# Moving the copy of the finished attention chunk out of PSUM from VectorE to ScalarE, in a fused attention and feed-forward kernel

## What is computed

```python
q = rope((x @ Wq + bq).reshape(B, T, 16, 64))
k, v = split(((x @ Wdown + bdown) @ Wup + bup).reshape(B, T, 16, 128))
att = softmax(einsum('bthd,btgd->bthg', q, rope(k)) / 8)      # heads h against heads g
out = einsum('bthg,btgd->bthd', att, v).reshape(B, T, 1024)
x = layernorm(x + out @ Wout + bout)
h = silu(x @ wg.T) * (x @ wu.T)                               # hidden size 3072, int weights / 127
x = layernorm(x + h @ wd.T)
```

## Time and profile before

| | us |
|---|---|
| time, median of 2 runs | 3666.14 (3661.13 to 3671.15) |
| the profiled execution: its time | 3658.49 |
| its span (core 7, the slowest) | 3656.6 |
| spans of the 8 cores | 3622.4 to 3656.6 |
| mean granted TensorE clock of the cores | 0.904 to 0.915 |

### The profile page before, as it was taken

The page is one execution under the profiler, slowest core; times in us unless marked ns, Lnnn a source line. Parts: engine busy times, 40 slices in busy tenths (PEclk is TensorE's granted clock), DMA queues, the critical chain, the costliest instruction groups (busy, mean ns, idle before and its releaser), DMA issues.

```text
span 3656.6 us, 41977 instructions; the slowest of 8 cores (3622.4 to 3656.6 us)
## 1 busy us (share of the span) xinstructions
PE 2749.2 (75%) x12672; PEld 1091.5 (30%) x12672; DVE 1726.1 (47%) x2582; ACT 768.6 (21%) x1349; POOL 292.1 (8%) x540
## 2 busy tenths in 40 slices
PE   0000686779887989698978997898879897989576
PEld 0000222233333333333333333333333333333222
DVE  1221446465546545654546364645565446545312
ACT  0000310133123220413040403231233113220101
POOL 0111000001000110011001100010001100110010
PEclk9999756699998999899999999899999998999778
DMA  6887100202232223222231224122322322222222
GB/s 186 241 240 198 34 1 24 58 29 64 87 78 67 67 93 76 72 59 87 71 91 50 78 74 111 35 62 92 81 67 64 93 61 70 67 87 69 87 72 84
DMA packets 108705, 303.97 MB, mean 83 GB/s; under 512 B 16192, under 2 KB 24768, under 8 KB 108496
## 3 DMA queue, kind: packets, MB, share of 16 engines
q1 hardware_dynamic: 61520, 169.14, 16.3%
q0 software_dynamic: 46976, 132.15, 12.3%
HBM read 269.77 MB, written 39.85 MB: 85 GB/s over the span
## 4 chain that ended last, share of the span: by engine, by line
PE 61%; DMA 9%; DVE 9%; issue 6%; ACT 4%; DVEq 0%; ACTq 0%; POOLq 0%; POOL 0%; SPq 0%
PE P L448 10%; PE P L395 9%; PE P L405 9%; PE P L731 9%; PE P L747 8%; PE P L644 7%; PE P L585 3%; DMA wgb<-wg_s 3%; DVE p_sb L696 3%; DMA wub<-wu_s 3%; PE P L344 2%; DMA wqb<-wq_s 2%; PE P L785 2%; DVE esum L670 2%; DVE hadb L619 1%
## 5 line engine op out<-in xcount | busy, mean ns | idle before, releaser
L696 DVE TENSOR_TENSOR p_sb<-P,vdup 128x512 bf16<-128x512 f32 x1024 | 698.4, 690 | 366.7 <-PE P L747 328.3
L395 PE MATMUL P<-x_bf,wgb 128*128 128x512 bf16 x1536 | 521.7, 409 | 106.7 <-DMA wub<-wu_s 85.9
L405 PE MATMUL P<-x_bf,wub 128*128 128x512 bf16 x1536 | 517.7, 406 | 18.3 <-DVE h_sb L421 18.2
L731 PE MATMUL P<-e_sb,selz_sb 16*128 16x512 bf16 x1024 | 427.2, 425 | 130.0 <-DVE e_sb L680 68.8
L448 PE MATMUL P<-h_sb,wdb 128*128 128x512 bf16 x1536 | 501.2, 391 | 19.6 <-DVE r_bf L457 19.0
L747 PE MATMUL P<-p_sb,id_sb 128*128 128x256 bf16 x2048 | 494.2, 299 | 24.1 <-DVE p_sb L696 17.9
L619 DVE TENSOR_TENSOR hadb<-q_sb,krep 128x2048 bf16<-128x2048 bf16 x256 | 310.0, 1224 | 373.2 <-PE P L644 284.8
L644 PE MATMUL P<-hadb,selred_sb 128*16 128x256 bf16 x2048 | 321.8, 276 | 42.4 <-DVE hadb L619 19.3
L311 PE MATMUL P<-x_bf,wd_sb 128*128 128x512 bf16 x128 | 38.9, 459 | 358.8 <-DMA x_bf<-xt 358.6
L414 ACT ACTIVATE s_sil<-P 128x512 bf16<-128x512 f32 x192 | 114.4, 596 | 921.9 <-PE P L395 921.3
L421 DVE TENSOR_TENSOR h_sb<-s_sil,P 128x512 bf16<-128x512 bf16 x192 | 130.5, 680 | 320.7 <-PE P L405 274.8
(11 more groups left out here) (69 smaller groups left out, 1936.0 us busy)
## 6 DMA issues: line engine op xcount, KB each, us to landing
wdb<-wdn_s SPq DMA_DIRECT2D x64, 768.0 KB, 4.5
wgb<-wg_s POOLq DMA_DIRECT2D x192, 256.0 KB, 3.0
wub<-wu_s POOLq DMA_DIRECT2D x192, 256.0 KB, 3.0
wob<-wout_s SPq DMA_DIRECT2D x128, 256.0 KB, 3.0
wqb<-wq_s SPq DMA_DIRECT2D x64, 256.0 KB, 3.0
yt<-x2b SPq DMA_DIRECT2D x64, 256.0 KB, 2.3
stg<-wg SPq DMA_DIRECT2D x24, 512.0 KB, 5.3
stg<-wu SPq DMA_DIRECT2D x24, 512.0 KB, 5.0
```

The lines of the kernel that those rows point to most:

```text
L395: e.matmul(o, l, r, start=st, stop=sp)),
L405: e.matmul(o, l, r, start=st, stop=sp)),
L696: add('V', (lambda e, o=o, a=a, b=b: e.tensor_mul(o, a, b)), waits=w, inc=s_v, d=640)
L731: e.matmul(o, l, r, start=True, stop=True)),
```

## The change

The copy from P7 to `avn` is no longer a `tensor_copy` on VectorE: it is an `activation` with the function Identity on ScalarE, counted by ScalarE's semaphore `s_s`. All that waited for the copy now waits for that semaphore. Three waits that stood for more than the copy are moved to the last product of the AV stage (`avtt_end`), because that is what frees P5 and P6: the guard of half 1's k matmuls, the P5/P6 guard of the second output projection (`erep_end`) and the wait of the next step's head. VectorE's count per chunk is 8, not 9. The copy's entry in the scheduler's table stays 510 ns.

```diff
--- before.py
+++ after.py
@@ -302,8 +302,8 @@
                     if m == 0:
                         w.append(xcast_c[c])
                         if c == 0:
-                            if ck['avn_h1']:
-                                w.append((s_v, ck['avn_h1']))
+                            if ck['avtt_end'][1]:
+                                w.append((s_v, ck['avtt_end'][1]))
                     o = P[5 + m][:, :]
                     l = wd_sb[:, m * 1024 + c * 128:m * 1024 + (c + 1) * 128]
                     r = xb[:, c * ST:(c + 1) * ST]
@@ -657,8 +657,8 @@
                 NPRE = 25
                 v_norm0 = v0 + 17
                 v_norm = v0 + NPRE
-                v_tt = lambda J, gp: v0 + NPRE + J * 9 + gp + 1
-                v_avn = lambda J: v0 + NPRE + (J + 1) * 9
+                v_tt = lambda J, gp: v0 + NPRE + J * 8 + gp + 1
+                avn_s = lambda J: sc0 + J + 1
 
                 exp_g = lambda g: exp_end - NH + g + 1
                 add('V', (lambda e, o=esum32[:, :], a=e_sb[:, 0:HF],
@@ -697,11 +697,13 @@
                             waits=w, inc=s_v, d=640)
                     o = avn[:, J * HF:(J + 1) * HF]
                     i_ = P[7][:, 0:HF]
-                    add('V', (lambda e, o=o, i=i_: e.tensor_copy(o, i)),
-                        waits=[(s_pe, pe_gsum(J, NH - 1)), (s_v, s_v.c)], inc=s_v)
+                    add('S', (lambda e, o=o, i=i_:
+                              e.activation(o, i, AF.Identity)),
+                        waits=[(s_pe, pe_gsum(J, NH - 1)), (s_s, s_s.c)],
+                        inc=s_s, d=510)
                 ck['avtt_end'][hf] = v_tt(XC - 1, 7)
-                prev_avn_end = s_v.c
-                erep_end = prev_avn_end
+                prev_avn_end = s_s.c
+                erep_end = v_tt(XC - 1, 7)
                 for J in range(XC):
                     sched = [('b', 0), ('b', 1), ('b', 2), ('g', 0), ('g', 1)]
                     for gp in range(3, 8):
@@ -736,18 +738,18 @@
                                 w.append((s_v, v_tt(J, g // 2)))
                             if g == 0:
                                 if J >= 1:
-                                    w.append((s_v, v_avn(J - 1)))
+                                    w.append((s_s, avn_s(J - 1)))
                                 elif hf == 0:
                                     w.append((s_s, kv_evac_g[-1]))
                                 else:
-                                    w.append((s_v, prev_avn_end_hf0))
+                                    w.append((s_s, prev_avn_end_hf0))
                             o = P[7][:, 0:HF]
                             r = p_sb[(g // 2) % 2][:, (g % 2) * HF:(g % 2 + 1) * HF]
                             add('T', (lambda e, o=o, r=r, st=(g == 0), sp=(g == NH - 1):
                                       e.matmul(o, id_sb[:, :], r, start=st, stop=sp)),
                                 waits=w, inc=s_pe, d=152)
                 assert s_pe.c == pe0 + XC * 24
-                assert s_v.c == v0 + NPRE + XC * 9
+                assert s_v.c == v0 + NPRE + XC * 8
                 prev_av_pe_end = s_pe.c
                 if hf == 0:
                     prev_avn_end_hf0 = prev_avn_end
@@ -770,7 +772,7 @@
                 for m in range(XC):
                     w = [(s_ld[m % 2], ld0[m % 2] + 16 * (m // 2 + 1))]
                     if m == 0:
-                        w.append((s_v, avn_end))
+                        w.append((s_s, avn_end))
                         w += p56_guard
                     if m < 2:
                         if prev_wout_v[0]:
@@ -805,7 +807,7 @@
             vd0 = plan_kv_part(0, 1)
             exp_end0, had0 = plan_sc(0, kd0)
             avn_end0, erep_end0 = plan_av(0, exp_end0, vd0)
-            kd1 = plan_kv_part(1, 0, guard=[(s_v, avn_end0)])
+            kd1 = plan_kv_part(1, 0, guard=[(s_v, ck['avtt_end'][0])])
             vd1 = plan_kv_part(1, 1)
             exp_end1, had1 = plan_sc(1, kd1)
             wo0 = plan_wo(0, avn_end0, [(s_s, exp_end1)])
```

## The result

The changed kernel took 3596.27 us (median of 11 runs), the kernel before, run beside it on the same chip, 3704.36 us (median of 10). The ratio that the comparison gives is 0.9786 (95% interval 0.9753 to 0.982), 2.1% faster; it and all that follow leave out executions in which the cores of a die ran at a lowered clock, which is why it is not the ratio of the two medians. The forecast was 1.2% faster with 3560 to 3680 us around it: the time lies inside, but the gain is 1.8 times what the sum gave. A gain of over 2% it left to rival B, with a chance of 0.15; the interval reaches from 1.8% to 2.5%, so on which side of 2% the change lies is open. The profiled execution took 3587.69 us against 3658.49.

What follows compares the result with a forecast made beforehand. TensorE's work and what makes it wait were taken as the bound. Gains 4 + 4 + 14 + 10 + 6 + 3 = 41 us, loss 1, gave 3618.5 from 3658.5, put at 3622 as median; range 3560 to 3680.

Steps and rivals of the forecast that it cites:

- rival B: Whole kernel: clock up at once at both AV starts, holes close, border and other waits go; 102 us, about 3560; chance 0.15.
- The copy at a border, 4 us: Between chunks the copy runs beside an equally long broadcast, its twin; without it the product starts little sooner, gain 4 us.
- The start of half 0, 14 + 10 us: TensorE's 3.12 us wait before broadcast 2 (the hole) is filled by eleven matmuls, 14 us; clock rises sooner, 10 us.
- the clock should rise sooner with eleven in a row; I take half: Start of half 0's AV stage: of 19 us lost to the clock in six steps, 10 us are regained.
- Half 1, 6 + 3 us: Start of half 1's AV stage: smaller clock fall, 6 us; no wait for the eviction behind the copy, 3 us.
- 0.83 (3.4 us lost) and 1.00, middle 1.7 us: Half 1's first 20 us: clock loss per step taken midway between two readings, 12 us in seven steps, half regained.
- Between the halves, 4 us for the guard: Half 1's first k matmuls wait for the last product, not the copy; of 4.6 us waiting, 4 counted as gain.
- Losses, 1 us: ScalarE: changes between Silu and exponential grow from 100 to 102, counted as a loss of 1 us (0 to 3).
- Rival A: Whole kernel: only the copy counts, moved matmuls are missed elsewhere, clock goes its own way; about 3657 us; chance 0.27.
- Rival C: Half 0's borders lacking feed-forward matmuls: clock falls, 3.4 us each; at 40 of 98 borders about 3755 us; chance 0.08.
- Right: Confirming signs: 128 ScalarE copies of 0.38 us, products 0.2 to 0.4 us sooner, 3.12 us wait under 0.5, clock above 0.85.
- Wrong: Refuting signs: waits for products beyond 80 us, half 0's clock below 0.9 outside its first chunk, or table loads at copies.

Runs made afterwards that it cites:

- experiment 3: Half 0's start, five steps: eight up matmuls moved into the wait in the old kernel, 0.9968; moved back in the changed kernel, 0.9877; first 16 moved in old, 1.0003.

## Why the prediction was right, and where it was not

- *The copy at a border, 4 us*: right. Chunks 2 to 7 together became 0.4 us shorter in each half, some 5 us over 13 halves, and step 0 stayed as it was. From the end of a chunk's last product to the next product, mean over the five borders from chunk 2 on in steps 2 to 7: 1.42 to 1.10 us in half 0, 1.40 to 1.18 in half 1, within the 0.2 to 0.4 forecast; with the copy on ScalarE in the old order 1.37 and 1.34. With the new order and the copy on VectorE it is 1.20 and 1.24 us, so most of the shortening is the order's. The twin broadcast is what counts. TensorE gained little of it, as said.
- *The start of half 0, 14 + 10 us*: right in size (23.8 us), but by luck, since its parts were wrong. The 1.00 taken as the good end of the clock came from a window that starts 6.7 us late; from the first product of that stage it is 0.83 on the same core. As the mean of the cores the clock of the first 20 us was 0.73 in steps 2 to 7 and became 0.95. By the prediction's own arithmetic that is 4.4 us a step and 27 us in six steps, where 10 were put, and the hole's 14 us can't stand beside it. The filled hole is worth 0.3% in the old order and 0.9% in the new one. The step "the clock should rise sooner with eleven in a row; I take half" left out that matmuls put there are missing elsewhere, which experiment 3 shows to cancel the gain in the old order.
- *Half 1, 6 + 3 us*: the mechanism was right (the eviction behind the copy, and the clock that falls behind it), the size too small by a factor of three: 29.2 us. The failing step is "0.83 (3.4 us lost) and 1.00, middle 1.7 us". No row shows a half 1 at 1.00; the 1.00 was a window of half 0 (on the slowest core two of the seven steps do have 1.00 in half 1). As the mean of the cores the clock of half 1's first 20 us was between 0.82 and 0.88 in every one of the seven steps, 0.85 in all, and became 0.99: 2.9 us a step or 20 us by the same arithmetic, where 6 were put. The wait for the eviction was 8.7 us in the seven stages and is 0.7, where 3 were put. Against this, chunk 2 lost 7 us.
- *Between the halves, 4 us for the guard*: the guard came as forecast (3.4 us of waiting gone as the mean of the cores), but the term for the weights was missing. The waits for weights, 85.9 us over the span of the kernel before, were not in the sum, though the new order moves the very matmuls that wait. They carried 23 of the 27.7 us.
- *Losses, 1 us*: too small. Head and softmax stages grew by 16 us. In the head stage there are not more feed-forward matmuls (90 and 88 on core 5 in seven steps) and not more waits (106 and 105 us), but the granted clock is lower, 0.950 against 0.967. In half 0's softmax one h product now stands ahead of seven scalings in steps 2 to 4, 6 and 7, and this stage grew by 3.9 us in the seven steps. The table loads at the Silu are 51, one more, which fits the forecast of two more changes in all. No experiment took these 16 us apart, so why the head's clock is lower is open.
- In sum the mechanisms were mostly right and the size was not; that the time lies in the range owes something to its width of 120 us. 40 us forecast, 71.5 measured as the mean of the cores (70.8 between the two profiled executions). The step from one to the other: half 1 +20, between the halves 28 less 4, the end of the step +7, the losses -15, and the 4 us of the borders, which lie inside the AV stages and can't be counted twice.
- Rival A (only the copy counts) is out: the order alone gives 1.65%. Rival B had the right signs but put 41 us on the borders, which gave some 5. Rival C (clock falls at borders) came in part, but in half 1 and not in half 0, where the prediction looked: the clock of chunk 2 was below 0.9 in 22 of 56 stages, and chunk 2 grew by 7 us over the seven steps as the mean of the cores. Half 0 was at 1.00 from chunk 1 on in all 56. Experiment 3 made such a fall in half 0, after 5.2 us without feed-forward matmuls, and it cost 3.1 us in chunk 1 of the five edited steps (12.70 against 9.63), near the 3.4 per fall that the rival was priced at.
- Of the signs, all under "Right" came: 128 copies of 0.38 us, the wait ahead of the third broadcast gone in the five steps, the clock behind it 0.95, no sum that waits for a copy. None under "Wrong" did: the waits for products are 66.5 us, and no table load stands at a copy. The signs did not cover half 1's chunk 2 and the weights.

## What to carry to other kernels

When a short instruction is moved off an in-order queue, look at what stands behind it and who feeds TensorE from there, not at its own length: here 0.42 us in seven places were worth 0.6%, and the same 0.42 us in the other 121 places some 0.2% in the old order, less than the intervals can tell. With a list scheduler in the kernel, a change of engine is first a change of order; write the order out as a table and try both halves of the change alone before crediting either. And when moving filler work into a hole, count what is left for the stretch behind it; before all that, look for waits that a shared semaphore makes, like the one between paired weight loads: without it the old kernel was 2.6% faster, against 2.1% by this change.

## What the runs showed that I had not expected

- Small edits of the order move the granted clock, and with it more time than the moved instruction takes. Seven times one exchanged pair of instructions took half 1's clock in its first 20 us from 0.85 to 0.95 (cores 4 to 7).
- A fall of the clock can move instead of going away: in half 1 it went from chunk 1 (49 of 56 stages before) to chunk 2 (22 of 56 after).
- Filling 3.1 us of idle time with useful matmuls, five times, together with the next few matmuls moved forward, gave 1.0003: the clock came up sooner, and fell again within 10 us.
- With the two weight transfers of 256 KB issued 0.53 us apart, the second landed 3.2 us after its issue (median), against 3.0 us with 3.5 us between them: they hardly slow each other here. By these medians the pair is there after 3.7 us instead of 6.5.
